# Router logits of a mixture-of-experts block: transposes and a DVE sum replaced by fp32 matmuls that ACT reads from PSUM

## The reference, cut to what matters

```python
logits = x @ gate_w.T                       # (4096, 8)
scores = jax.nn.sigmoid(logits)
scores_c = scores + correction_bias
...
topk_idx = jax.lax.top_k(scores_for_choice, TOPK)[1]
topk_w = jnp.take_along_axis(scores, topk_idx, axis=-1)
topk_w = topk_w / (jnp.sum(topk_w, axis=-1, keepdims=True) + 1e-20)
...
y = jnp.einsum('eni,eih->enh', jax.nn.silu(g) * u, Wd)
out = routed + _mlp(x, Wg_s, Wu_s, Wd_s)
```

## Time and profile before

| what | value |
|---|---|
| median of 3 runs | 721.54 us (719.54 to 724.91) |
| the profiled execution | 724.91 us |
| its span, first to last instruction | 722.9 us |
| PE, DVE, ACT, POOL busy | 614.8, 452.5, 277.2, 177.5 us |
| mean granted clock of TensorE | 0.934 |

### The profile page before, as it was taken

The page is one execution under the profiler, slowest core; times in us unless marked ns, Lnnn a source line. Parts: engine busy times, 40 slices in busy tenths (PEclk is TensorE's granted clock), DMA queues, the critical chain, the costliest instruction groups (busy, mean ns, idle before and its releaser), DMA issues.

```text
span 722.9 us, 10596 instructions
## 1 busy us (share of the span) xinstructions
PE 614.8 (85%) x3352; PEld 479.4 (66%) x3352; DVE 452.5 (63%) x892; ACT 277.2 (38%) x501; POOL 177.5 (25%) x177
## 2 busy tenths in 40 slices
PE   3674968688977977877667999999999999999997
PEld 2553745456544754554245888888888888888886
DVE  3677656877487758861268384766647575665653
ACT  2432447244643456343442343424232243324222
POOL 2152004310351005200110233232423223232222
PEclk9866989999989999999957999999999999999999
DMA  7750133514244333554212103121211203121220
GB/s 250 186 134 24 37 80 89 126 43 97 53 114 93 74 74 86 115 160 136 62 34 74 45 17 92 39 92 55 87 59 62 84 1 102 44 88 59 75 73 30
DMA packets 39856, 58.65 MB, mean 81 GB/s; under 512 B 7984, under 2 KB 21040, under 8 KB 39792
## 3 DMA queue, kind: packets, MB, share of 16 engines
q1 hardware_dynamic: 39824, 58.25, 29.2%
HBM read 31.76 MB, written 4.85 MB: 51 GB/s over the span
## 4 chain that ended last, share of the span: by engine, by line
PE 36%; issue 32%; DVE 13%; POOL 8%; DMA 5%; SPq 2%; ACT 2%; DVEq 1%; POOLq 0%; ACTq 0%
PE pg L1467 5%; PE py L1482 4%; PE pu L1467 4%; POOL hl L1174 4%; PE oT L938 4%; PE smax L877 3%; PE sT L918 3%; DMA qs<-mt 3%; PE oT L942 3%; DVE mx L604 2%; SPq L296 2%; POOL d L399 2%; PE work L822 2%; DVE mx L632 2%; PE work L953 1%
## 5 line engine op out<-in xcount | busy, mean ns | idle before, releaser
L1174 POOL TENSOR_TENSOR hl<-sg,hh 128x512 fp32r<-128x512 f32 x72 | 93.4, 1298 | 243.6 <-ACT hh L1217 234.3
L503 ACT ACTIVATE ex<-sT 128x512 f32<-128x512 f32 (+1 forms) x160 | 91.9, 593 | 158.0 <-PE sT L918 132.9
L1211 ACT ACTIVATE sg<-pg 128x512 f32<-128x512 f32 x72 | 43.1, 599 | 196.3 <-PE pu L1467 196.2
L877 PE MATMUL smax<-km,qs 96*128 96x308 f32 (+1 forms) x244 | 87.2, 393 | 25.9 <-DVE mx L604 19.0
L604 DVE TENSOR_REDUCE mx<-smax 128x2 f32<-128x308 f32 x185 | 80.8, 471 | 35.3 <-PE smax L877 34.1
L877 PEld LDWEIGHTS smax<-km,qs 96*128 96x128 f32 x244 | 49.0, 210 | 59.3 <-DVE mx L604 34.8
L1482 PE MATMUL py<-wxl,hh 128*128 128x256 f32 x288 | 81.4, 283 | 3.4 <-DVE x L1361 2.2
L1482 PE MATMUL py<-wxh,hl 128*128 128x256 f32 x288 | 80.5, 279 | 0.0
L1482 PE MATMUL py<-wxh,hh 128*128 128x256 f32 x288 | 80.3, 279 | 0.0
L1349 DVE TENSOR_TENSOR sg<-cwb,sg 128x512 f32<-128x512 f32 x64 | 60.5, 945 | 10.9 <-DMA cwb<-cwt_d 8.0
L918 PE MATMUL sT<-qs,ks 128*128 128x256 f32 (+1 forms) x128 | 54.0, 439 | 13.4 <-DMA qs<-mt 12.1
(11 more groups left out here) (155 smaller groups left out, 1116.7 us busy)
## 6 DMA issues: line engine op xcount, KB each, us to landing
cwb<-cwt_d SPq DMA_DIRECT2D x64, 256.0 KB, 3.4
qs<-qh SPq DMA_DIRECT2D x64, 128.0 KB, 2.5
qs<-ql SPq DMA_DIRECT2D x32, 128.0 KB, 2.4
at<-rden_d SPq DMA_DIRECT2D x64, 64.0 KB, 2.2
out<-x SPq DMA_DIRECT2D x8, 512.0 KB, 4.4
ks<-km SPq DMA_DIRECT2D x16, 231.0 KB, 3.7
wx<-in_wx SPq DMA_DIRECT2D x9, 384.0 KB, 5.7
x<-in_x SPq DMA_DIRECT2D x3, 1024.0 KB, 8.5
```

Of the source, the lines that this page charges most:

```text
L503: nc.scalar.activation(ex[:, g % 2, i % 5, q0:HALF], ST[i % 2][:, q0:HALF], ACT.Exp).then_inc(exp_s, 1)
L877: last_one = nc.tensor.matmul(bank[:, 0:width], qs[0:96, s, tile * P:(tile + 1) * P], km[:, s, 0:width], start=True, stop=True)
L1174: nc.gpsimd.tensor_tensor(hl[:, i % R, :], sg[:, i % R, :], hh[:, i % R, :], ALU.subtract).then_inc(hl_done, 1)
L1211: nc.scalar.activation(sg[:, i % R, :], PG[i % RG][:], ACT.Silu).then_inc(sg_s, 1)
```

## The change

PE no longer transposes `lgT`. It multiplies each 128-token piece of `lgT` (as the stationary operand, 16 rows by 128 columns) by the first eight columns of `expert` (as the moving operand, 16 x 8), in plain fp32, which transposes and adds the two halves in one step. DVE's `logits_in` and the tile `lgs` go, with their semaphore. ACT's `scores` waits for PE (`lg_ps`) and reads `PM` itself. The nop ahead of PE's step goes. The order of all else stays, and `weights_T`, the next to write `PM`, still waits for `sc_s`, which ACT gives.

```diff
-    lgs = sb("lgs", [P, TB, E])
...
-    lg_s = sem("logits_set")
...
         def scores(n):
-            act.wait_ge(lg_s, n + 1)
+            act.wait_ge(lg_ps, n + 1)
             act.wait_ge(route, NROUTE * n)
-            nc.scalar.activation(sc[:], lgs[:], ACT.Sigmoid)\
+            nc.scalar.activation(sc[:], PM[:, 0:TB * E].rearrange("p (t e) -> p t e", t=TB), ACT.Sigmoid)\
                 .then_inc(sc_s, 1)
...
-        def logits_in(n):
-            dve.wait_ge(lg_ps, n + 1)
-            dve.wait_ge(sc_s, n)
-            nc.vector.reduce_sum(lgs[:], PM[:, 0:2 * TB * E].rearrange("p (t r e) -> p t e r", t=TB, r=2), AX_X)\
-                .then_inc(lg_s, 1)
...
-            if ahead and e == 4:
-                logits_in(n + 1)
...
-                logits_in(0)
...
             pe.wait_ge(misc_free, 4 * n + 4)
-            pe.nop().then_inc(waited, 1)
             for j in range(TB):
-                last = nc.tensor.transpose(PM[:, 2 * j * E:2 * (j + 1) * E], lgT[:, j * P:(j + 1) * P],
-                                           con("ident", 0, 2 * E)[:, 0:2 * E])
+                last = nc.tensor.matmul(PM[:, j * E:(j + 1) * E], lgT[:, j * P:(j + 1) * P],
+                                        con("expert", 0, 2 * E)[:, 0:E], start=True, stop=True)
             last.then_inc(lg_ps, 1)
```

## The result

The changed kernel takes 728.36 us (median of 8 runs, 726.80 to 732.47), the kernel before 723.91 (8 runs beside them, 719.54 to 725.62). The medians are 4.5 us apart (0.61%). The ratio, which goes by all runs and not by the medians, is 1.0077, 95% interval 1.0047 to 1.0105; of 723.91 us that is 5.6 us, between 3.4 and 7.6. So the change is slower by some 4.5 to 5.6 us: less than the 1% that was called a difference, but the interval excludes no change. The profiled execution took 730.77 us, its span is 728.7.

What follows compares the result with a forecast made beforehand. PE's instruction stream was taken to bound the kernel from 410 us on, busy 304.6 of 308 us. Loads 4.5, nop 0, DVE and ACT 0, block 0 0.9 gave +5.4 on 721.54: 726.9 us, range 722.0 to 731.0.

Steps and rivals of the forecast that it cites:

- Part 1: Logits step on PE: four transposes become eight load-and-matmul pairs, +0.64 us a block, +4.5 us in seven blocks.
- A: Logits step on PE: the eight loads don't overlap, +8.8 us in the loop, 732.5 us in all; chance 0.10.
- B: Logits step on PE: loads keep the transposes' 0.061 us pace and the nop's gap goes, 722.3 us; chance 0.12.
- Part 2: Ahead of PE's logits step: removing the nop is worth 0, bounds 0 and -1.4 us.
- Part 3: Behind the logits: DVE's reduction goes, ACT reads PSUM; sigmoid about 0.3 us later, under cover, value 0.
- Block 0: First block, at half clock: logits step 1.2 us longer and on the path, +0.9 us, between 0.6 and 1.4.
- Rival D: Block 0: fp32 matmuls in place of transposes let PE's clock rise sooner, giving back 0.9, 726.0 us; chance 0.10.
- Rival C: Loop: PE's residual wait absorbs the 0.64 and DVE's saving shortens it, not slower, 721.0 us; chance 0.08.

Runs made afterwards that it cites:

- e1: Kernel before with only the four fp32 matmuls in place of transposes; DVE still copies logits into lgs, nop stays: 727.78 us, ratio 1.0078.
- e6: Changed kernel with lgT and the table of ones in rounded fp32r, so four loads instead of eight: 727.17 us, ratio 1.0049.
- e5: Changed kernel with lgT given 128 rows instead of 16, still eight loads: 726.05 us, ratio 1.0034 to the kernel before.
- e3: Changed kernel with the nop put back ahead of the matmuls: 728.84 us, ratio 1.0072 to the kernel before.
- e7: Kernel before with lgT of 128 rows, four 128 x 128 transposes and no nop: 722.71 us, ratio 0.9998.
- e2: Kernel before without DVE's reduction; ACT reads the logits' high part from PSUM, low part left out, transposes and nop stay: 724.05 us, ratio 1.0003.
- e8: Changed kernel with both fp32r (four loads) and lgT of 128 rows: 724.95 us, ratio 1.0019 to the kernel before.
- e10: Kernel before with the changes of e7 and e9 together: 718.82 us, ratio 0.9930.
- e4: Changed kernel with the unused tile lgs still allocated, so later tiles keep their old addresses: 728.79 us, ratio 1.0065 to the kernel before.
- e9: Kernel before with DVE doing the previous block's residual ahead of the second item's products, not behind them: 718.73 us, ratio 0.9954.
- e11: Changed kernel with the residual moved first on DVE: 723.82 us, ratio 1.0015 to the kernel before.

## Why the prediction was right, and where its parts were off

**Direction and size.** Forecast 726.9 from a base of 721.54, +5.4 us or +0.75%; measured ratio 1.0077, and 4.5 us between the medians. The later runs moved the base to 723.9, so that the changed kernel's median came out at 728.36 and not at 726.9. That the total fits so closely is partly luck, as the parts show.

**Part 1, the loads.** Eight loads 0.11 apart, 0.99 us against 0.35: measured 0.99, and +0.64 a block by the step (1.534 - 0.894), in each of seven blocks: 4.5 us. e1 shows that this part is the whole cost, e6 that the price goes by the number of loads. Reading the count of calls against the count of records (two per fp32 matmul) and the one bare pair of loads in the same stretch was enough. Rivals A and B are out: 0.11 is neither 0.188 nor 0.061.

The Trainium skill, "TensorE: Matmul & The Clock Gate", section "LDWEIGHTS (loading the stationary operand)", prices a load by columns: e5 and the changed kernel, with 128 and 16 rows, agree in that the rows don't matter to the spacing (0.11 in both), and 107 ns fits it. It does not cover the loads of the 16-row transposes, 0.061 apart, nor the 0.21 at granted clock 0.50, nor the gaps that e5 removed.

**Part 2, the nop.** Value 0, as predicted; e3 shows it. That the gap of this step is the change to a 16-row operand is shown by e5 and e7, where it goes; L839's own gap, with 32 columns, was the row that suggested it and was not tried.

**Part 3, DVE and ACT.** Value 0, as predicted: e2. The sigmoid chain moved by 0.34 us against 0.3 predicted, under a cover of 1.5. One reading there was too short: PE's loads wait not only for the residual but, in every profile, once for POOL's hl near the end of the program (1.3 us), with or without the change.

**Block 0, +0.9.** The step there grew by 1.29 us (gate matmuls at 1.80 us behind the first logits matmul, against 0.51), more than the 1.2 taken: the two loads 0.17 apart were the wrong row, the eight are 0.21 apart, and the upper bound of 0.22 was right. What the clock gives back depends on its course, and the course differs from profile to profile in two places. One is the pause near 392 us, before the items begin. In the kernel before PE restarts from it at low clock (the busy times are PE, PEld, DVE, ACT, POOL):

```profile
390.20:394.20 4.00, 0.00 (x0) 0.00 (x0) 3.95 (x5) 0.00 (x0) 0.00 (x0) 0.79 0.57 183
394.20:399.30 5.10, 5.02 (x12) 3.99 (x13) 4.24 (x7) 0.63 (x1) 1.37 (x1) 0.50 0.21 51
```

and in the changed one at full clock, falls, and is back sooner:

```profile
393.30:395.30 2.00, 0.96 (x4) 0.85 (x5) 1.97 (x5) 0.30 (x1) 0.00 (x0) 1.00 0.00 0
395.40:398.80 3.40, 3.40 (x10) 2.65 (x9) 3.11 (x5) 0.23 (x1) 1.37 (x1) 0.51 0.22 77
```

The other is the stretch ahead of the router's matmuls. It is at low clock in the changed kernel and at full clock in e3, which has the same instructions but for the nop (PE alone):

```profile
368.30:371.50 3.20, 1.11 (x4) 0.50 0.40 114
```

```profile
366.90:370.10 3.20, 0.66 (x4) 1.00 0.32 82
```

This second place doesn't go with the change: both kinds of clock occur there with four loads and with eight. The first place does, as far as these profiles go. The block 0 column, sorted by both:

| clock ahead of the router | four loads | eight loads |
|---|---|---|
| low | before 48.94, e6 49.26, e8 49.18, e10 48.81: all restart at low clock | changed 49.02, e1 48.92, e4 48.86, e5 48.94: all restart at full clock |
| full | e2 47.62, e7 47.81, e9 47.55: restart at full clock | e3 48.54, e11 48.28: restart at full clock |

In the upper row the eight loads cost nothing (means 49.05 and 48.94 us). The kernel before and the changed one show how. The rise comes 16.4 and 16.6 us behind the first transposition, nearly the same moment in spite of the longer queue, so 0.5 of the 1.29 comes back, as the prediction had it: the gate-up matmuls end 0.76 us later, and the items begin 0.76 later (29.17 and 28.41 us behind the first transposition). Then the kernel before runs its first items at low clock for 5.1 us and the changed one for 3.4, which gives the rest back. The attention projection ahead of the pause ends 24.3 to 24.6 us behind the first transposition in before, e6 and e8, and 24.9 to 25.1 in the four with eight loads; the pause is 4.1 us long in all. That the later end is what keeps the clock up is argued from this order, not shown.

In the lower row the means are 47.66 and 48.41: block 0 pays 0.75 us, or 0.8 against e2 and e9 alone, since e7's full-height transposes take 0.26 longer there. So the forecast's +0.9 and its mechanism fit one course of the clock, and the other pays nothing, by a step that the prediction did not have. There is one profile of each kernel, so how often each course occurs is not known.

Rival D, a clock that rises sooner because matmuls replace transposes, has nothing for it: the rise comes 6.3 us behind the first logits load before (375.98) and 6.6 after (375.23). Its result, block 0 for nothing, is nevertheless that of the upper row, by the restart behind the pause and not by the rise.

**What no term held.** The down slots, 118.4 instead of 117.0 ns, 1.0 us in six blocks by e2 and e11: a tile less in SBUF moved all the tiles behind it by 128 bytes. I had costed the missing tile at nothing without saying so. Why an address makes the slot 1.4 ns longer stays open; only that it goes with the address is shown.

**The sum again.** 4.5 + 0 to 0.8 for block 0 + about 1.2 (seven blocks of longer down slots) is 5.7 to 6.5 us, inside the interval (3.4 to 7.6 us) and above its middle of 5.6. The forecast's 5.4 was near because block 0 was put too high for some courses of the clock and the addresses at nothing. Without the address part e1 should cost 4.5 to 5.3 us, and its ratio says 5.6. The times don't settle the last microsecond.

**Rival C.** Excluded twice: e2 (no gain from DVE's side) and e11 (no cover for PE's side). The 1.6 us wait in one block of the changed profile isn't the change's either: e1, e3 and e4, with eight loads, have none over 0.9, while e5 has one and e7, with transposes, has two. In that block the four normalising instructions of DVE take 2.45 us, 1.39 in others, behind POOL's rstd:

```profile
604.43 2.45 DVE L1263 TENSOR_SCALAR xn<-x,mv,rstd 128x256 f32 x4 [1.00 <-POOL rstd L1166]
```

The long waits of e5 and e7 come with the same 2.4 us. What makes them long there was not tried.

## What to carry to other kernels

On an engine that is 99% busy, count records, not calls: one fp32 matmul is two loads and two matmuls, a transpose is one of each (at nearly half the spacing with 16 rows and 16 moving columns, at the same with 128 of each), and work taken off a waiting DVE pays for none of it. With short moving operands the weights set the price, 0.11 us for each 128-column load at full clock and 0.21 at half, and a 16-row operand among 128-row ones costs another 0.3 us in gaps, which zero rows that are already there can remove. Look at what the critical engine waits for before trimming what waits for it: a reorder of two DVE instructions gave 0.5% in the kernel before and, against the changed kernel, 0.6% in e11, more than any form of this step.

## What the runs showed of the hardware that I had not expected

- A tile of 128 bytes a partition more or less in front changes the slot of 256-column fp32r matmuls by 1.4 ns (117.0 and 118.4), in eleven profiles without an exception; with 32 bytes in its place it is 118.0 and 118.1 in two more.
- Changing from 128-row to 16-row operands and back costs 0.3 us of PE (1.534 against 1.241 for the same eight loads, 0.2 ahead and 0.1 behind); the prediction had seen the gaps, but not that full-height operands would remove both.
- An idle time on the weight-load row overstates the loss: 0.77 a wait shown on the mean, 0.6 a block gained when it was removed.
- The loads of fp32 transposes have no single spacing: 0.061 us with 16 rows and 16 moving columns, 0.11 with 128 of each (e7). Rows and columns were changed together and are not told apart.
- A longer step at low clock can cost nothing in the end: in profiles that agree ahead of the router, 0.76 us more queue ahead of a pause of 4.1 us went with 1.7 us less of low clock behind it.
